# Second graph convolution of a four-layer network: nine of 26 source columns by one-hot rows in three groups of three, with masks and picks moved

## What is computed

```python
w = jax.nn.relu(efeat @ W1 + b1) @ W2 + b2
w = w.reshape(E, IN_DIM, OUT_DIM)
msg = jnp.einsum('ei,eio->eo', h[src], w)
agg = jax.ops.segment_sum(msg, dst, num_segments=N)
```

## Time and profile before

| what | us |
|---|---|
| median of three runs | 9060.25 (9060.18 to 9061.02) |
| the profiled execution, its own time | 9049.36 |
| its span on the core | 9047.6 |
| stage nnconv, first gather issued to last scan | 1438.7 to 3016.2 |
| TensorE, VectorE, ScalarE, GpSimd busy over the span | 81%, 85%, 49%, 74% |

### The profile page before, as it was taken

The page is one execution under the profiler, slowest core; times in us unless marked ns, Lnnn a source line. Parts: engine busy times, 40 slices in busy tenths (PEclk is TensorE's granted clock), DMA queues, the critical chain, the costliest instruction groups (busy, mean ns, idle before and its releaser), DMA issues. The chain is left out here.

```text
span 9047.6 us, 135625 instructions
## 1 busy us (share of the span) xinstructions
PE 7287.6 (81%) x35152; PEld 4135.0 (46%) x35152; DVE 7667.6 (85%) x11882; ACT 4453.0 (49%) x7248; POOL 6665.2 (74%) x6335
## 2 busy tenths in 40 slices
PE   3778765888888258888888889578888888888884
PEld 2666653555555135555555555323333333333331
DVE  7999984777777468888888888589999999999997
ACT  4666664666666146666665556323333333333333
POOL 5777777777777577777777777377777777777774
PEclk9888886888888579999999999789999999999997
DMA  4222221112111111111111111122222222222223
GB/s 148 59 59 59 59 53 35 44 45 46 45 44 45 20 24 32 28 32 29 31 29 31 28 32 20 16 62 80 75 75 81 76 75 75 82 75 75 76 81 98
DMA packets 499695, 493.19 MB, mean 55 GB/s; under 512 B 181075, under 2 KB 396906, under 8 KB 498731
## 3 DMA queue, kind: packets, MB, share of 16 engines
q1 hardware_dynamic: 299595, 371.60, 12.2%
q0 software_dynamic: 199904, 119.78, 9.7%
HBM read 240.96 MB, written 249.95 MB: 54 GB/s over the span
## 5 line engine op out<-in xcount | busy, mean ns | idle before, releaser
L2494 POOL DMA_INDIRECT attn_got<-tab,attn_line x1760 | 2111.3, 1200 | 582.6 <-issue 499.4
L1954 POOL DMA_INDIRECT sheaf_got<-tab,sheaf_idx x1612 | 1710.3, 1061 | 490.0 <-issue 474.0
L2547 PE MATMUL attn_q<-attn_X,ident 128*128 128x512 f32 x3520 | 1743.8, 635 | 3.3 <-DVE attn_X L2719 1.8
L2043 PE MATMUL sheaf_acc<-sheaf_hot_hi,sheaf_wide 128*128 128x392 bf16 x6696 | 1356.9, 345 | 279.5 <-DVE sheaf_hot_hi L2246 276.1
L1479 POOL DMA_INDIRECT nnconv_got<-tab,nnconv_idx x1116 | 1082.0, 970 | 402.1 <-issue 335.1
L2547 PEld LDWEIGHTS attn_q<-attn_X,ident 128*128 128x128 f32 x3520 | 678.2, 204 | 1085.7 <-issue 1085.7
L1168 POOL DMA_INDIRECT gcn_got<-tab,gcn_idx x868 | 901.8, 1039 | 317.9 <-issue 279.2
L2680 DVE TENSOR_TENSOR attn_T<-attn_w,attn_got 128x1024 f32<-128x1024 f32 x880 | 1034.8, 1217 | 79.6 <-DVE attn_T L2712 34.1
L2043 PEld LDWEIGHTS sheaf_acc<-sheaf_hot_hi,sheaf_wide 128*128 128x128 bf16 x6696 | 656.4, 106 | 816.5 <-issue 488.4
L2624 ACT COPY attn_S<-attn_q 128x512 f32<-128x512 f32 x440 | 255.9, 582 | 1559.8 <-PE attn_q L2556 1559.8
L1257 PE MATMUL gcn_acc<-gcn_hot,pieces 128*128 128x512 f32 x2604 | 752.3, 448 | 268.7 <-DVE gcn_hot L1191 267.2
(11 more groups left out here) (503 smaller groups left out, 13356.6 us busy)
## 6 DMA issues: line engine op xcount, KB each, us to landing
sums<-attn_S SPq DMA_DIRECT2D x110, 1024.0 KB, 4.2
tops<-attn_S SPq DMA_DIRECT2D x110, 512.0 KB, 3.0
attn_got<-tab,attn_line POOLq DMA_INDIRECT x1760, 2.5
sheaf_got<-tab,sheaf_idx POOLq DMA_INDIRECT x1612, 2.5
gcn_key<-src_key SPq DMA_DIRECT2D x62, 384.0 KB, 3.7
gcn_blk<-src_blk SPq DMA_DIRECT2D x62, 384.0 KB, 4.2
nnconv_got<-tab,nnconv_idx POOLq DMA_INDIRECT x1116
nnconv_key<-src_key SPq DMA_DIRECT2D x62, 256.0 KB
```

What stands on the lines that cost most here:

```text
L1954: e.indirect_dma_start(out=got[at.b][:, j, D:D + T2], out_offset=None, in_=tab[2], in_offset=indices(idx[at.b], j)).then_inc(s_got[half][a ...
L2043: mm = e.matmul(pacc[k][:, 0:HH], wide[at.b][half][:, part, col, :], hot[:, k * HH:(k + 1) * HH], start=False, stop=False, skip_group_chec ...
L2494: e.indirect_dma_start(out=got[at.b][:, 4 * q + n, :], out_offset=None, in_=tab[3], in_offset=indices(ids[:, q, n, :], D + 2)).then_inc(s_ ...
L2547: e.matmul(to, ident[:, :], X[:, q, :, n, :], start=n == 0, stop=False)
```

## The change

JN goes from 18 to 17, so that nine columns come by one-hot rows, in three groups of three (384 edges) in place of two groups of four (512). `BY_ACT` becomes (7, 5, 0): ScalarE makes the rows of group 0 and five of group 1, VectorE two of group 1 and all seven of group 2. On TensorE a group's `picked` stands right ahead of the next group's `summed`. On VectorE the masks of groups 1 and 2 stand between `times` and the totals; chosen(k+1, 2) comes behind totals 0 and 1. On ScalarE moved(k, 2) is added at the end of the step.

```diff
-        GN = 2
-        BY_ACT = (NC, 4)
-        JN = J - GN * GW
+        GN, GC = 3, 3
+        BY_ACT = (NC, 5, 0)
+        NA2 = sum(1 for n in BY_ACT if n > 0)
+        ND2 = sum(1 for n in BY_ACT if n < NC)
+        JN = J - GN * GC
...
-            key = [sbl(f"key{b}", [P, GN, GW * P], F16) for b in range(2)]
-            blk = [sbl(f"blk{b}", [P, GN, GW * P], F16) for b in range(2)]
-            hot = [sbl(f"hot{q}", [P, NC, GW * P], F32R) for q in range(2)]
-            held = [sbl(f"held{q}", [P, GW * P]) for q in range(2)]
+            key = [sbl(f"key{b}", [P, GN, GC * P], F16) for b in range(2)]
+            blk = [sbl(f"blk{b}", [P, GN, GC * P], F16) for b in range(2)]
+            hot = [sbl(f"hot{q}", [P, NC, GC * P], F32R) for q in range(2)]
+            held = [sbl(f"held{q}", [P, GC * P]) for q in range(2)]
...
-                        turn_wait(e, s_hot, at.of(GN, g + 1))
+                        if BY_ACT[g] > 0:
+                            turn_wait(e, s_hot, at.of(NA2, g + 1))
                         if BY_ACT[g] < NC:
-                            turn_wait(e, s_chosen, at.of(1, 1))
+                            turn_wait(e, s_chosen, at.of(ND2, g))
...
-                                mm = e.matmul(pacc[:, :],
+                                mm = e.matmul(pacc[:, 0:GC * P],
...
-                        for j in range(GW):
-                            at_col = q * GW * 2 * D + j * 2 * D
+                        for j in range(GC):
+                            at_col = q * GC * 2 * D + j * 2 * D
...
                         matrices(at, 1)
                         if more:
                             picked(nxt, 0)
+                            summed(nxt, 1)
                         matrices(at, 2)
                         if more:
-                            summed(nxt, 1)
+                            hidden(nxt, 0)
                         matrices(at, 3)
                         if more:
-                            hidden(nxt, 0)
+                            picked(nxt, 1)
+                            summed(nxt, 2)
                         matrices(at, 4)
                         if more:
-                            picked(nxt, 1)
+                            hidden(nxt, 1)
                         matrices(at, 5)
+                        matrices(at, 6)
                         if more:
-                            hidden(nxt, 1)
-                        matrices(at, 6)
+                            picked(nxt, 2)
                         if at.k < NB - 2:
                             summed(at.plus(2), 0)
...
                         rectified(at, 1)
                         if more:
                             chosen(at.plus(1), 1)
+                        moved(at, 2)
...
-                                               in1=pacc[:, :], op0=ALU.is_equal, op1=ALU.mult).then_inc(s_mask, 1)
+                                               in1=pacc[:, 0:GC * P], op0=ALU.is_equal, op1=ALU.mult).then_inc(s_mask, 1)
...
                                 times(at, g)
+                            if more and pair[0] in (2, 4):
+                                mask(at.plus(1), pair[0] // 2)
                             for g in pair:
                                 added[g] = total(at, g)
-                            if more and pair[0] == 2:
-                                mask(at.plus(1), 1)
+                            if more and pair[0] == 0:
+                                chosen(at.plus(1), 2)
                             if at.k < NB - 2 and pair[0] == 4:
                                 chosen(at.plus(2), 1)
```

More of the change, by code:

```diff
@@ L1587, in moved @@
                         e.wait_ge(s_sel, at.of(GN, g + 3))
-                        e.copy(got[at.b][:, JN + g * GW:JN + (g + 1) * GW, :].rearrange("p j f -> p (j f)"),
-                               psel[:, q * GW * 2 * D:(q + 1) * GW * 2 * D]).then_inc(s_moved, 1)
+                        e.copy(got[at.b][:, JN + g * GC:JN + (g + 1) * GC, :].rearrange("p j f -> p (j f)"),
+                               psel[:, q * GC * 2 * D:(q + 1) * GC * 2 * D]).then_inc(s_moved, 1)
                     def rectified(at, q):
@@ L1646, in step @@
                             chosen(at.plus(1), 1)
+                        moved(at, 2)
                     for q in range(QT):
                         rectified(At(0), q)
-                    for g in range(GN):
+                    for g in range(2):
                         chosen(At(0), g)
                     flagged(At(0))
-                    for g in range(GN):
-                        moved(At(0), g)
-                        chosen(At(1), g)
+                    moved(At(0), 0)
+                    moved(At(0), 1)
+                    chosen(At(1), 0)
+                    moved(At(0), 2)
+                    chosen(At(1), 1)
                     step(At(1))
@@ L1746, in _ @@
                     chosen(At(0), 1)
+                    chosen(At(0), 2)
                     for g in range(GN):
```

## The result

The changed kernel takes 9213.7 us (median of four runs, 9211.2 to 9216.8) against 9060.2: 1.7% slower, ratio 1.0170 (1.0152 to 1.0188), or +153 us. The forecast was +302, so the sign was right and the size half of it.

What follows compares the result with a forecast made beforehand. A ring of waits between VectorE and TensorE was taken as the bound. (29.6 - 24.64) x 60 = 298, plus 4 before the first block, gave +302: 9351 profiled, 9362 as median; own range 9290 to 9430, 8 in 10 9125 to 9540.

Steps and rivals of the forecast that it cites:

- The gather is worth nothing here: GpSimd: one gather less a block, 79 us in all, worth nothing while VectorE and TensorE's waits keep blocks slower than 23.9.
- Rival C: GpSimd's gathers are the bound after all: block at its pace of 22.6 us, -124 us, 8936; chance 5%.
- VectorE's work: Per block on VectorE: three masks for two add 0.3 us, nine rows for three 1.8; its work becomes 22.2 us.
- TensorE's sum at either clock: TensorE's sum of a 384-edge group: 2.6 us at the full clock, 4.6 at the low clock.
- The new order: At full clock, a whole sum stands behind mask 1 ahead of matrices 4; times 4 waits 2.8 us, next scan at 25.6.
- rival A: TensorE's clock stays full in the chain behind mask 1: block 25.8 us, +74 us, 9134; chance 8%.
- The low clock: TensorE behind mask 1: 8.9 us at low clock end matrices 5 3.8 us later; block 29.6 us after adding 0.2.
- Rival B: TensorE's clock falls more often, the block's first half running low too: block 33.9 us, +556 + 4, 9620; chance 15%.

Runs made afterwards that it cites:

- matrices first: Changed kernel with matrices 4 and 5 on TensorE ahead of the picks and the sum of group 1 to 2: 8914.2 us, ratio 0.9846.
- late masks: Changed kernel with the masks of groups 1 and 2 back behind the totals of their pair: 9564.5 us, ratio 1.0567.
- light-first version: Changed kernel with matrices 4 and hidden 1 between the picks and the sum of group 1 to 2: 9367.2 us, ratio 1.0355.
- moved rows: Changed kernel with the two one-hot rows of group 1 made by ScalarE in place of VectorE: 9203.0 us, ratio 1.0166.

## Why the prediction was right in its sign and off in its size

- *The gather is worth nothing here:* right. GpSimd waits 222 us for the bias copies and is at 61% in place of 73%. Rival C is out for this order, but became the truth once the order was mended: with matrices first the block is 22.58, the 22.6 that C gave.
- *VectorE's work:* right. Seven rows of 384 take 2.32 us (2322.52 to 2324.84), 0.33 each, as taken; a mask 0.53. The estimate of 0.36 that the Trainium skill gives (VectorE: DVE Perf Modes, the table of cycles) is 9% above that.
- *TensorE's sum at either clock:* right. 2.60 at the full one (2.6 was taken), 4.18 with 3.4 of them at the low one, and 4.76 wholly at it in the version with late masks (4.6 was taken).
- *The new order:* right step for step. Times 3 no longer waits, the idle ahead of the picks is 3.25 (3.2), the first part of the chain is as laid out, and with the idle filled the block is 25.72 at a clock of 0.97, against 25.8 forecast as rival A. One reading on the way was wrong: mask 2 was said to come about 11 us later in the block than mask 1 did before, where the forecast's own times give 7 (19.7 for 12.6) and the trace 9. It carried no cost: VectorE waits for such a load once in the stage, 12 us, as before.
- ***The low clock* is the step that failed.** It took the 8.9 us a block of before as one stretch and put all of it on the chain, 3.8 us of delay. The rows show two stretches of 3.4 us, with one on the chain: the sum takes 1.6 us longer, and hidden and both matrices nothing. In a block, 25.6 + 3.8 + 0.2 was forecast and 25.72 + 1.48 measured. (29.6 - 27.2) x 61 = 146 us, which is nearly all of the miss of 149. The mean of a state was carried over to an order with other work behind the fall. Before, matrices 5, hidden and matrices 6, all small products, came first behind it and stretches lasted 6.8 or 10.2 us; the light-first version brings 6.8 us and more back by the order alone. That is not the only way to a long stretch, as the versions with moved rows and with late masks show, and what sets its length stays open.
- *Rival B* had the second fall right in kind, at an idle of 1.83 us ahead of the picks of group 2, and wrong in price: what lies behind it is in time for mask 0 and times 0. The rule of the Trainium skill (TensorE: Matmul & The Clock Gate, on psum-queue depth-cycling) agrees with these rows in so far as the clock does go down and up twice a block; but with the longest idle filled, idles of 1.85 and 2.36 us are left, and the clock falls 22 times, for 3.4 us each, in the 39 blocks between 1800 and 2800 us. So short idles alone did bring the clock down here, though in some blocks only and not twice in each.

## What to carry over

A block of work that has to wait for another engine should not stand ahead of work that could already run: list for each wait what is queued behind it and move ahead whatever has its inputs. Take an engine's load away only after the order lets that engine set the pace: the same step from 18 gathers to 17 cost 153 us in one order and won 100 in the other. Where TensorE's clock falls in or behind an idle, ask which instructions come right behind it, and measure after filling one idle whether the fall has moved to the next.

## What was not expected of the hardware

Filling TensorE's idle with products nobody reads made the changed kernel 90 to 99 us faster and the kernel before 51 us slower; two fills made the latter 52 us faster. A stretch at the 1.2 GHz level lasted 3.4 us in the changed kernel, and 6.8 us when matrices and hidden were put between the picks and the sum; but it also lasted 6.8 us with the order untouched and two rows moved to ScalarE, where the clock fell 2.2 us ahead of the picks. And 0.66 us less work on VectorE in a block was worth 3 to 11 us in all while the clock fell, 42 us with the idle filled, since the low stretch then covered the picks too and cost 0.61 us more.
